# Unit-matrix products between the gate's products of the second router

## The reference

```python
def _L1_ffn_ref(x, Wr, W1, b1, W2, b2):
    x_flat = x.reshape(-1, dim)              # layernorm(x) comes in: 2048 x 256
    logits = x_flat @ Wr                     # 2048 x 8, the gate
    w, ind = jax.lax.top_k(logits, K)        # K = 2
    w = jax.nn.softmax(w, axis=-1)
    combine = jnp.einsum('tke,tk->te', jax.nn.one_hot(ind, E, dtype=x.dtype), w)
    def body(acc, params):                   # over the 8 experts
        W1e, b1e, W2e, b2e, ce = params
        h = jax.nn.gelu(x_flat @ W1e + b1e, approximate=False)
        y = h @ W2e + b2e
        return (acc + ce[:, None] * y, None)
    ...
```

## Time and profile before

| | |
|---|---|
| median of 3 runs | 721.01 us (718.66 to 725.44) |
| the profiled execution | 727.21 us |
| its span | 724.9 us |
| PE busy | 678.3 us, 94% |
| DVE, ACT, POOL busy | 474.1, 464.8, 294.0 us |
| mean granted clock of PE | 0.97 |
| DMA | 104.97 MB, mean 145 GB/s |

### The profile page before, as it was taken

One profiled execution on the slowest core, in us unless ns is written; L12 is line 12 of the kernel. 1 busy time (PEld: TensorE's weight loads), 2 busy tenths in 40 slices (PEclk: granted clock), 3 DMA queues, 4 the chain that ended last, 5 costly groups with the idle time before them and its releaser, 6 DMA issues.

```text
span 724.9 us, 21812 instructions
## 1 busy us (share of the span) xinstructions
PE 678.3 (94%) x7522; PEld 577.3 (80%) x7523; DVE 474.1 (65%) x1188; ACT 464.8 (64%) x1178; POOL 294.0 (41%) x221
## 2 busy tenths in 40 slices
PE   4889899989978999999999989999999999999992
PEld 4434467668868899998999978885899999999992
DVE  4898578774758776666654559956897455454541
ACT  2466679745558878777766538850997665656661
POOL 1101135434724454544655422402265555545432
PEclk9999899999999999999999999859999999999997
DMA  8981101215358847699796559944555444443431
GB/s 265 374 280 40 30 1 32 88 37 168 147 181 264 189 76 166 165 231 239 193 210 129 88 138 405 372 174 176 141 105 84 70 83 80 71 82 65 79 52 23
DMA packets 110679, 104.97 MB, mean 145 GB/s; under 512 B 53067, under 2 KB 96085, under 8 KB 109734
## 3 DMA queue, kind: packets, MB, share of 16 engines
q1 hardware_dynamic: 95654, 83.80, 37.9%
q0 software_dynamic: 14976, 20.58, 17.8%
HBM read 64.84 MB, written 28.23 MB: 128 GB/s over the span
## 4 chain that ended last, share of the span: by engine, by line
PE 76%; DVE 8%; DMA 5%; ACT 3%; issue 3%; POOL 2%; SPq 1%; POOLq 0%; ACTq 0%; DVEq 0%
PE bank L1262 9%; PE bank L1260 9%; PE bank L1261 9%; PE bank L1273 9%; PE bank L1274 9%; PE bank L1275 9%; PE bank L1381 2%; PE bank L997 2%; PE bank L1410 2%; DMA out<-x_arena,add_now 1%; PE bank L1150 1%; POOL weights L837 1%; DMA x_arena<-token_rows,gather_now 1%; PE bank L1167 1%; PE bank L999 1%
## 5 line engine op out<-in xcount | busy, mean ns | idle before, releaser
L1584 ACT ACTIVATE work<-bank,b_cols 128x128 f32<-128x128 f32 x624 | 175.3, 381 | 134.9 <-PE bank L1262 128.2
L1260 PE MATMUL bank<-x_arena,weights 128*128 128x128 f16 x1248 | 213.2, 219 | 1.5 <-DVE x_arena L2069 0.7
L1261 PE MATMUL bank<-x_arena,weights 128*128 128x128 f16 x1248 | 213.2, 219 | 0.3 <-issue 0.3
L1262 PE MATMUL bank<-x_arena,weights 128*128 128x128 f16 x1248 | 213.2, 219 | 0.0
L2084 DVE TENSOR_TENSOR work<-work 128x512 f16<-128x512 f32 x156 | 100.9, 688 | 120.8 <-ACT work L1592 109.5
L1273 PE MATMUL bank<-weights,work 128*128 x624 | 170.2, 273 | 1.7 <-issue 0.7
L1275 PE MATMUL bank<-weights,work 128*128 x624 | 170.1, 273 | 0.0
L1274 PE MATMUL bank<-weights,work 128*128 x624 | 170.1, 273 | 0.0
L843 POOL DMA_INDIRECT x_arena<-token_rows,gather_now x78 | 85.3, 1094 | 150.7 <-DVE gather_now L2078 104.1
L1260 PEld LDWEIGHTS bank<-x_arena,weights 128*128 x1248 | 122.1, 98 | 2.7 <-DVE x_arena L2069 1.1
L1261 PEld LDWEIGHTS bank<-x_arena,weights 128*128 x1248 | 122.1, 98 | 1.2 <-issue 0.4
(11 more groups left out here) (249 smaller groups left out, 1214.2 us busy)
## 6 DMA issues: line engine op xcount, KB each, us to landing
weights<-in_L_ffn_W SPq DMA_DIRECT2D x76, 256.0 KB, 7.7
raw<-in_L_ffn_W SPq DMA_DIRECT2D x44, 256.0 KB
split_dram<-row_arena SPq DMA_DIRECT2D x12, 512.0 KB
weights<-split_dram SPq DMA_DIRECT2D x3, 2048.0 KB, 15.5
odd_sum<-padding_row SPq DMA_DIRECT2D x1, 2176.0 KB, 13.2
token_rows<-row_arena SPq DMA_DIRECT2D x1, 2072.0 KB, 7.7
x_arena<-in_x SPq DMA_DIRECT2D x4, 512.0 KB, 6.5
weights<-in_L_ffn_sW SPq DMA_DIRECT2D x8, 256.0 KB, 7.2
```

The costliest lines, as they stand in the source:

```text
L1260: nc.tensor.matmul(o, w1_at[f][c][0].block(), hi, start=c == 0, stop=False)
L1261: nc.tensor.matmul(o, w1_at[f][c][0].block(), lo, start=False, stop=False)
L1262: m = nc.tensor.matmul(o, w1_at[f][c][1].block(), hi, start=False, stop=c == DC - 1)
L1584: m = nc.scalar.activation(hid[:, k, f * P:f * P + P], h_ps[k][half][:, g * P:g * P + P], ACT.Gelu, bias=b1_cols[n][:, f, bass.ds(e, 1)], ...
```

## The change

`router_logits1` gets unit-matrix products into bank 7: three ahead of the wait of its first call, one between the two tiles of each call (behind the second product of the even tile), and one behind each call, after the signal that the gate's products are done. With eight calls that is 3 + 8 x 2 = 19 products of 512 columns. Nothing else is changed.

```diff
@@ -1403,12 +1403,17 @@
                 m.then_inc(router_tp_done, 1)
 
             def router_logits1(b, h):
+                if (b, h) == (0, 0):
+                    keep_clock(bank[7], 3)
                 pe.wait_ge(router_xlnT_ready, half_no(b, h))
                 for t in range(2 * h, 2 * h + 2):
                     i = TB * b + t
                     for c in range(DC):
                         m = nc.tensor.matmul(logits1_ps(i)[:, 0:E], router_xlnT[:, b % 2, c, t * P:t * P + P], gate_cols[:, 1, c, :], start=c == 0, stop=c == DC - 1)
+                        if t % 2 == 0 and c == DC - 1:
+                            keep_clock(bank[7], 1)
                 m.then_inc(xlnT_used, 1)
+                keep_clock(bank[7], 1)
 
             for h in range(2):
                 turned1(0, h)
```

## The result

| | before | after |
|---|---|---|
| median of 20 runs | 724.89 us (718.66 to 729.13) | 721.29 us (716.84 to 725.20) |
| ratio | | 0.9959, 95% interval 0.9939 to 0.9979 |
| profiled execution, its span | 727.21, 724.9 us | 725.11, 722.9 us |

The change makes the kernel 0.41% faster, 3.0 us (1.5 to 4.4), where 4.4 us and 716.6 us had been forecast. The time is inside the stated range and the direction is right; the size is not. Most of the miss in absolute time (721.29 for 716.6, 4.7 us) is the reference point: the three runs of before had a median of 721.01, twenty have 724.89, 3.9 us more. The runs of each kernel spread over 8 to 10 us, and why they do is what the rest of this document is about.

A forecast was written before the change was run, and what follows sets the result against it. PE's chain at the low clock bounds the second router. With the clock up, PE is 3.4 us sooner at the last gate products; with DVE's 1.0 us of slack, 4.4 us off the 721.01 median gives 716.6, range 714.5 to 725.5.

The forecast's parts named there:

- What bounds the router: Second router, 464.25 to 489.11 us: the chain of waits stays on PE, which runs mostly at 1.2 GHz.
- The sum with the clock up: First gate products to the counts' reader: if the clock stays up, the reader and all behind it move 4.4 us sooner.
- the price of a product: Each added product between gate products: 0.22 us at the full clock, 0.435 at the low; bounded below by half of 0.22.
- Three products ahead of the first: Ahead of the first gate products: 0.66 us of products in 0.74 us of PE idle time, costing nothing.
- The thin place: Ahead of batch 2's gate products: ACT writes high parts before the read-out, so PE idles about a microsecond.
- case A: Second router: the clock stays up throughout, gaining 4.4 us, for 716.6 us; chance 0.42.
- Rival B: Second router: the clock falls once ahead of batch 2, some 3.4 us, and returns in batch 3; gain 2.7, 718.3; chance 0.26.
- Rival C: Second router: the clock falls near 466.5 and stays low to 484; added products cost 6.4 us, 727.4; chance 0.15.
- D: Second router: the clock falls early and comes back halfway, low for 7 to 10 us; 720 to 722, no change; chance 0.17.
- The prediction's own sign: Forecast is wrong if 464.25 to L1969 isn't at least 3 us shorter than 24.9, or the end doesn't move.
- break-even of 8.8 us: Second router: each microsecond at half clock costs half a microsecond, so the gain is gone after 8.8 us of it.
- Transposes: Start of the kernel: the clock rose after almost only f32 transposes, so they count, against the Trainium skill's rule; not certain.

The follow-up runs named there:

- the filled gap: Four unit-matrix products added to the changed kernel ahead of the wait of batch 2's first gate products, with one register operation more a tile: 717.38 us, ratio 0.9973.
- the control: The kernel before with one register operation more a tile on PE's sequencer, against the kernel before: 722.71 us, ratio 1.0036.

## Why the prediction was right or wrong, point by point

**What bounds the router: right.** PE's chain at the low clock. Give it the full clock (the filled gap) and the stretch shrinks from 24.86 to 19.74 us, where DVE and not PE reaches the counts last.

**The sum with the clock up: right, a little low.** Forecast 4.4 us; three stretches at 1.00 measure 19.73, 19.73 and 19.74, which is 5.1 less. The 0.7 us are spread over three terms. Batch 2's gate products start 9.26 us after the first in the profile that held (463.99 to 473.25), not 9.60: the prediction left ACT's work of batch 2 where it stood, and with PE faster it begins sooner. From there to DVE's copy it is 6.51 us and not 6.75, and DVE needs 3.96 to the counts and not 4.1. The term that was most mis-sized is the price of a product, and little of it shows: seven or eight products at half their price save 0.8, but 0.3 is lost again at batch 3, where transposes and read-out take 1.29 us (476.09 to 477.38) and 0.97 had been allowed. Four gate records and the product behind them take 0.57 us at the full clock (461.10 to 461.67 in the kernel with the filled gap), where sixteen records alone took 1.95, 0.45 to 0.49 for four: about 0.1 us a product, not 0.22. At the low clock it is 479.08 - 477.99 = 1.09 in the profile after, for 0.85: 0.24, not 0.435. It is the lower end of the bound, and for the reason given there. PE's weight loads in the kernel with the filled gap:

```profile
461.46 0.63 PEld L1416 LDWEIGHTS bank<-gate_cols,weights 128*128 128x128 f32 x4
```

The next gate weights begin to load at 461.46, together with the unit product and 0.21 us ahead of the gate product at 461.67. I took the nearest row, of the same instruction in a series, and it was the wrong neighbour. Three products ahead of the first: free, as forecast.

**The thin place: right, to the place.** The prediction named the microsecond ahead of batch 2's gate products, made by ACT's high parts; filling it or reordering ACT is what keeps the clock. In all four profiles of the changed router that lost the clock, and in the two with half of the products and the gap open, it fell 10.3 to 12.1 us after the first gate products, and the gap ends 9.27 us after them. With all products and the gap closed, by filling or by ACT's order, five profiles of five held it.

**"Forecast is A, 716.6": the step that failed.** The forecast took case A, the clock up, as what the kernel does, with B, C and D beside it as other fates of the kernel. They are fates of single executions, and 4.4 us is what one execution gains that holds the clock. The prediction's own sign shows the failure: the stretch was to be at least 3 us shorter than 24.9, and in the profile after it was 0.75 us longer. Six profiles of this router (the two with the 24 products exchanged among them) took 25.61, 23.98, 25.63, 25.61, 19.73 and 19.73 us: two of six hold the clock. The median is made of both kinds. With 5.1 us where it holds and between 0.9 gained and 0.8 lost where it falls, a measured gain of 3.0 needs about six in ten to hold, and the profiles show two in six. The clocks of the single runs give a larger count. With the gap filled every run had a mean clock of 0.984 or more, and none of the 24 runs of the control and of the products of 8 columns had more than 0.982. Of the changed kernel's runs 13 of the 20, and 5, 5 and 7 of the three times 12, are at 0.984 or more: 30 of 56. As an estimate, 0.65 x 5.1 less 0.35 x 0.35 (the mean loss of the four that fell) is 3.2 us for the 20 runs, and 2.6 with the share of all 56; 3.0 was measured. The mark is not sharp, since low stretches elsewhere shift it: 4 of 35 runs of the unchanged kernel on the first chip reach 0.984, and 5 of 24 with ACT's order mended don't. The other half of this step is where the gain was put: on 721.01, a median of three runs that twenty runs place at 724.89.

**Rival B: its trigger right, its price wrong for this kernel.** It said one dip of 3.4 us, a loss of 1.7, a gain of 2.7, with the dense run of unit products and transposes of batch 3 to bring the clock back. When the clock fell it stayed low for 13.6 us (472.1 to 485.7) or 10.2 (after 472.8), through batch 3, and the stretch came out at +0.75 or -0.9. It came back only at the end of the low parts or just behind them (485.7, 483.0). So B's trigger had C's end. B as told does occur with the eight products between the tiles alone: down at 470.1, back at 473.5.

**Rival C: its price right in kind.** It never came from the start in a profile, but its mechanism is what the fallen runs show: with half of the router at the low clock the added products eat most of what the later fall saves (0.93 gained, 0.70 lost from batch 2 on), but the 0.98 behind them, where the low parts now run at the low clock to their end, is a term that the prediction doesn't have. Its break-even of 8.8 us at the low clock was low: at 10.2 the stretch still gained 0.9. The gain with the clock up is 5.1 and not 4.4, and a microsecond at the low clock cost 0.41 to 0.43 us ((5.1 - 0.9) / 10.2 and (5.1 + 0.75) / 13.6) and not 0.5, which puts it near 12.

**Transposes: the trace's side was right, its evidence weaker than told.** The rise at the start of the kernel was read from the durations of the earlier trace rows. The granted clock of the same stretch, which the prediction doesn't give, doesn't show it:

```profile
11.00:12.00 1.00, 1.00 (x7) 1.00 (x6) 0.00 (x0) 0.00 (x0) 0.00 (x0) 1.00 0.22 47
```

It reads 1.00 from the start on, while the transposes there take 0.22 us each, twice their time at 21.17. One of the two is not what it seems, and no run tells which. So rows 9 alone don't show that transposes raise the clock; for holding it the 48 transposes are the evidence, where clock and pace agree. The Trainium skill ("TensorE: Matmul & The Clock Gate", Part 4) says that transposes don't count as busy the same way; for f32 transposes these runs don't agree.

**Measurement: half seen.** I put the gain on a median of three runs although the profiled one lay 6.2 us above it. Their spread goes with the same effect (time and clock correlate at 0.85 and 0.83): low stretches that come or don't at several thin places (near 46, 80, 208, 425 to 437, 495 us in one profile or another), 0.25 to 0.5 us for each microsecond at the low clock.

What stays open: why the same instruction stream holds the clock in one execution and not in another; no run here varied that. And how many of the 16 products are needed once the gap is closed: eight were not told apart from all in the median, and the one profile of that kernel did lose the clock early, for 3.4 us.

## What to carry to other kernels

Where a stage is thin for TensorE, look for its longest idle time first and fill that, since products there are free; products strung between the real ones cost about 0.1 us each even at the full clock. Better still, ask which engine made the gap: two calls exchanged on ScalarE made the router 0.9 us shorter than four products did, because they gave the idle time back too (the two kernels never ran on one chip, so their medians don't tell). And when runs of one program differ by more than the change is worth, read several profiles, and the mean granted clock of each run, before believing one: a change can move how often a stall happens, and its worth is then that share times the stall's price.

## What the runs showed of the hardware that had not been expected

- A unit product of 512 columns between f32 gate products costs about 0.1 us at 2.4 GHz and 0.24 at 1.2, about half of its 0.22 and 0.435 in a series.
- 48 f32 transposes of 128 x 128, 5.44 us with no other product among them, held the granted clock at 1.00; 5.5 us of idle time in their place lost it (one profile of each).
- The row table (32 products of 40 columns) takes no longer at a granted clock of 0.50 than at 1.00, 3.1 us, with DVE's parts as a possible second cause.
- Eight-column products and transposes, with two 512-column products a batch as before, held the clock for 7.5 us after the first gate products in one execution, where in two of the kernel before it fell within 2.4.
